# Attention as a 16-step pipeline per sequence, with the maxima as a 97th contraction row, in a one-core attention and mixture-of-experts layer

## The reference

```python
x = x + layernorm(attention(layernorm(x)))     # 16 query heads of 32, one key head and one value head, causal
x = x + layernorm(moe(layernorm(x)))           # 8 experts of 352, the best 2 per token, plus one shared expert of 1408
# attention: q = x @ q_w.T + q_b (16 heads); k, v = one head each
#   scores = q @ k.T / sqrt(32); keys after the query: -inf; softmax over keys; @ v; @ o_w.T + o_b
```

## Time and profile before

| | us |
|---|---|
| median of 3 runs (lowest, highest) | 2210.64 (2209.67, 2216.05) |
| the profiled execution, its own time | 2211.64 |
| the profiled execution, its span | 2209.9 |
| attention, routing, experts, shared expert and end | 0 to 829, to about 860, to 1445, to 2210 |
| busy in the span: TensorE, VectorE, ScalarE, GpSimd | 2059.7, 1141.1, 704.0, 465.8 |

### The profile page before, as it was taken

One profiled execution on the slowest core, in us unless ns is written; L12 is line 12 of the kernel. 1 busy time (PEld: TensorE's weight loads), 2 busy tenths in 40 slices (PEclk: granted clock), 3 DMA queues, 4 the chain that ended last, 5 costly groups with the idle time before them and its releaser, 6 DMA issues. The chain is left out here.

```text
span 2209.9 us, 32623 instructions
## 1 busy us (share of the span) xinstructions
PE 2059.7 (93%) x11754; PEld 1604.8 (73%) x11754; DVE 1141.1 (52%) x2253; ACT 704.0 (32%) x1254; POOL 465.8 (21%) x885
## 2 busy tenths in 40 slices
PE   5999999999999953799999999989999999999995
PEld 4666676766667633677788788878888888888884
DVE  4766758577675738444445555444433424334243
ACT  3425345353543420344444444332111111111111
POOL 1323414142341420211101111001012021120212
PEclk9999999999999975899999999999999999999998
DMA  5043261414415112444434545333022020220202
GB/s 172 31 119 114 62 174 38 136 54 120 128 48 153 39 57 79 172 156 154 154 141 180 211 143 195 109 105 100 19 76 95 19 76 19 76 95 19 76 20 95
DMA packets 104418, 222.76 MB, mean 101 GB/s; under 512 B 9472, under 2 KB 23552, under 8 KB 101152
## 3 DMA queue, kind: packets, MB, share of 16 engines
q1 hardware_dynamic: 92832, 184.14, 25.4%
q0 software_dynamic: 11520, 37.76, 5.4%
HBM read 157.37 MB, written 62.91 MB: 100 GB/s over the span
## 5 line engine op out<-in xcount | busy, mean ns | idle before, releaser
L1121 PE MATMUL ex_bank<-ex_xT,ex_gu 128*128 128x512 f32 (+14 forms) x1656 | 345.1, 367 | 5.4 <-DVE ex_xT L1155 5.4
L1121 PEld LDWEIGHTS ex_bank<-ex_xT,ex_gu 128*128 128x128 f32 (+1 forms) x1656 | 276.8, 182 | 69.9 <-DVE ex_xT L1155 5.9
L1171 DVE TENSOR_TENSOR sh_silu<-sh_silu,sh_bank 128x512 f32<-128x512 f32 x88 | 60.5, 688 | 444.6 <-ACT sh_silu L1164 444.6
L627 DVE TENSOR_REDUCE at_nmax<-at_bank 128x1 f32<-128x384 f32 (+3 forms) x512 | 216.5, 472 | 108.3 <-PE at_bank L431 108.2
L777 ACT ACTIVATE at_PT<-at_bank 128x512 f32<-128x512 f32 (+1 forms) x384 | 187.5, 526 | 265.0 <-PE at_bank L483 258.6
L1121 PE MATMUL sh_bank<-sh_xT,sh_gate 128*128 128x512 f32 x1056 | 256.3, 392 | 4.1 <-DVE sh_xT L1155 4.1
L1133 PE MATMUL sh_bank<-sh_dn,sh_act 128*128 128x512 f32 x1056 | 255.1, 390 | 0.0
L1121 PE MATMUL sh_bank<-sh_xT,sh_up 128*128 128x512 f32 x1056 | 253.9, 389 | 0.0
L837 POOL TENSOR_TENSOR at_minus_max<-idf,at_nmax 128x512 fp32r<-128x512 f32 x128 | 134.1, 1048 | 503.2 <-DVE at_nmax L627 484.9
L1164 ACT ACTIVATE sh_silu<-sh_bank 128x512 f32<-128x512 f32 x88 | 52.6, 598 | 586.4 <-PE sh_bank L1121 586.4
L1121 PEld LDWEIGHTS sh_bank<-sh_xT,sh_gate 128*128 128x128 f32 x1056 | 199.8, 189 | 45.9 <-DVE sh_xT L1155 4.3
(11 more groups left out here) (229 smaller groups left out, 2818.7 us busy)
## 6 DMA issues: line engine op xcount, KB each, us to landing
ex_gu_in<-gu_in SPq DMA_DIRECT2D x23, 1408.0 KB, 9.3
at_Qs<-q_dram SPq DMA_DIRECT2D x96, 256.0 KB, 5.7
ys<-sh_yk SPq DMA_DIRECT2D x17, 1024.0 KB, 5.7
q_dram<-at_q_h SPq DMA_DIRECT2D x64, 256.0 KB, 4.1
ex_dn_in<-dn_in SPq DMA_DIRECT2D x23, 512.0 KB, 9.9
at_x_in<-x_in SPq DMA_DIRECT2D x8, 1024.0 KB, 9.6
at_x_res<-x_in SPq DMA_DIRECT2D x8, 1024.0 KB, 6.6
x<-at_y SPq DMA_DIRECT2D x8, 1024.0 KB, 8.4
```

The costliest lines, as they stand in the source:

```text
L627: last = nc.vector.tensor_reduce(nmax[:, s % 3, i:i + 1], S_ps[u][:, col:col + (i + 1) * P], AX_X, ALU.max, negate=True)
L1121: last = self.nc.tensor.matmul(self.gate_up_ps[c % 2][which][0:m, 0:w], cols(i, k), self.xT[j][:, k, 0:w], start=(step == 0), stop=(step = ...
L1171: nc.vector.tensor_tensor(silu[c % 2][0:m, 0:w], silu[c % 2][0:m, 0:w], gate_up_ps[c % 2][1][0:m, 0:w], ALU.mult).then_inc(s["product"], 1)
```

## The change

It rewrites the attention stage as one pipeline: a turn is 16 steps, one per head, and every engine's stream has the same step structure. Work of one head is spread over steps s (scores, maxima), s + 1 (the maxima's way to a row), s + 2 (scores by key) and s + 3 (exponentials). Everything else of a turn is a "filler" in one of the 16 steps: it goes through one bank (`F_ps`), so that each filler waits until the one before it was taken. A turn b holds heads of sequence b, the output projection of b - 1, the transposes and projections of b + 1, and the router of b - 2, so ten turns are run for eight sequences (two, a loop, and four written out).

- The negated maxima [128 queries, 4] are transposed by TensorE, copied by ScalarE to a row (`row`), and moved by a DMA on ScalarE's queue into a 97th row of `Qs`; `KsT` has ones in its 97th row. The ones matmuls (L483), the diagonals (L837) and the mask matmul of the transposed scores (L479) go.
- GpSimd zeroes the exponentials of later keys instead (`affine_select`, two per head, 384 + 128 columns), and makes the low half of the mixed values in VectorE's place.
- Sums and values share one bank (`AV_ps`). The sums are transposed by VectorE in 32 x 32 blocks, one reciprocal of 16 columns is taken, and a second transpose spreads it.
- There are two copies of the keys, `KsS` for scores by query and `KsT` for scores by key, both moved by ScalarE's queue, when the old ones have been read. Queries are moved per quarter as heads become free.
- The halves of the transposed normalized x1 are stored to DRAM (`xnT`, 2 MB per sequence) and the shared expert loads them into two sets of buffers, in place of loading rows, transposing and splitting.

The diff, cut to its core:

```diff
+        SUM_STEP = {9: 0, 13: 1, 1: 2, 3: 3}
+        MIX_STEP = {10: 0, 14: 1, 2: 2, 4: 3}
+        Q_STEP = {12: 0, 13: 1, 15: 2, 0: 3}
...
         def turns(engine, turn):
-            turn(0, True, False)
-            with engine.Fori(1, NB - 1) as b:
-                turn(b, False, False)
-            turn(NB - 1, False, True)
+            turn(0)
+            turn(1)
+            with engine.Fori(2, NB - 2) as b:
+                turn(b)
+            for b in range(NB - 2, NB + 2):
+                turn(b)
...
+            def transpose_maxima(n, h):
+                pe.wait_ge(max_ready, 3 * (H * n + h) + 3)
+                nc.tensor.transpose(AV_ps[0:QT, 0:P], nmax[:, h % 2, :], idf[:]).then_inc(rows_ps, 1)
...
+            def key_scores(n, h, before):
+                if h == 0:
+                    pe.wait_ge(kT_moved, 48 * n + 48)
+                pe.wait_ge(row_moved[h % 2], 8 * H * n + 16 * (h // 2) + 16)
+                for tb, tiles in enumerate(T_UNITS):
+                    if has(before[0]):
+                        pe.wait_ge(pt_ready, 3 * (H * before[0] + before[1]) + tb + 1)
+                    for j, col in tiles:
+                        w = (QT - j) * P
+                        last = nc.tensor.matmul(T_ps[tb][:, col:col + w], KsT[:, j * P:(j + 1) * P], Qs[:, h, j * P:S],
+                                                start=((j, col) == tiles[0]), stop=((j, col) == tiles[-1]))
+                    last.then_inc(shifted, 1)
...
         @block.tensor
...
+            def turn(b):
+                for s in range(H):
+                    n, h = head(b, s, 1)
+                    if has(n):
+                        m, g = group(b, s - 1, SUM_STEP)
+                        k, f = group(b, s - 1, MIX_STEP)
+                        if g is not None:
+                            pe.wait_ge(sums_taken, C * m + g + 1)
+                        elif f is not None:
+                            pe.wait_ge(mixed_taken, C * k + f + 1)
+                        elif has(head(b, s, 2)[0]):
+                            pe.wait_ge(row_taken, H * head(b, s, 2)[0] + head(b, s, 2)[1] + 1)
+                        transpose_maxima(n, h)
+                    if has(b):
                         query_scores(b, s)
+                    first_filler(b, s)
+                    begin_values(b, s)
+                    second_filler(b, s)
+                    end_values(b, s)
+                    transpose_v(b, s)
+                    n, h = head(b, s, 2)
+                    if has(n):
+                        key_scores(n, h, head(b, s, 3))
...
+            def take_sums(b, s):
+                n, g = group(b, s, SUM_STEP)
+                if g is not None:
+                    dve.wait_ge(summed, C * n + g + 1)
+                    nc.vector.transpose(sums_T[:], AV_ps[:]).then_inc(sums_taken, 1)
...
         @block.vector
...
+            def turn(b):
                 for s in range(H):
+                    maximum(b, s, 0)
+                    norm_steps(b, s, 0)
+                    invert_sums(b, s)
+                    maximum(b, s, 1)
+                    norm_steps(b, s, 1)
+                    spread_inverses(b, s)
+                    first_low(b, s)
+                    maximum(b, s, 2)
+                    norm_steps(b, s, 2)
+                    second_low(b, s)
+                    take_sums(b, s)
+                    scale_mixed(b, s)
+                    take_v(b, s)
+                    norm_steps(b, s, 3)
...
+            def move_row(b, s):
+                n, h = head(b, s, 1)
+                if has(n):
+                    act.wait_ge(row_taken, H * n + h + 1)
+                    act.dma_start(Qs[QK:QK + 1, h, :].bitcast(F32),
+                                  row[:, h % 2, :].bitcast(F32)).then_inc(row_moved[h % 2], 16)
...
         @block.scalar
...
+            def turn(b):
+                for s in range(H):
+                    exponentials(b, s, 0)
+                    if s == 2 and has(b) and has(b - 1):
+                        act.wait_ge(shifted, 3 * H * b)
+                        move_k(b, KsT, kT_moved)
+                    take_row(b, s)
+                    high_mixed(b, s)
+                    exponentials(b, s, 1)
+                    move_row(b, s)
+                    first_high(b, s)
+                    exponentials(b, s, 2)
+                    second_high(b, s)
+                    if s == H - 1 and has(b + 1):
+                        act.wait_ge(scores, 3 * H * (b + 1))
+                        move_k(b + 1, KsS, kS_moved)
...
```

## The result

The changed kernel takes 2258.4 us (median of four runs, 2254.7 to 2263.0) against 2211.6 for the kernel before in the same comparison: a ratio of 1.0208, 95% interval 1.0192 to 1.0225, slower by 2.1%. The prediction was 2216.6, range 2180 to 2250. The profiled run spans 2261.2 us; it is the slowest of the four, 4.6 above their median.

The account below looks back on a forecast made before the run. TensorE's instruction stream was taken to bound attention and shared expert, with waits replacing its removed attention work. From 2211.6: +20.9 attention, -12.5 and -2.4 shared expert make 2217.6, less 1.0 to the median: 2216.6 us, range 2180 to 2250.

Parts of the forecast that it names:

- The step that failed: Attention: a falling TensorE clock was no separate case, low only around 20 us idling; longest predicted wait 2.4 us.
- steps 0: First step of an attention turn: keys land 2.4 us into it; with its query projection predicted 8.2 us.
- steps 12: Attention step with a query projection as filler, bound by the loop through VectorE's third maxima: predicted 5.94 us.
- the ends: Attention's first turn 72 us from 42.5, eighth 82, ninth 38, then 38.6 to routing; end 850.1, 20.9 later.
- The steady schedule: Attention's full turns: sixteen step lengths, each worked out from waits and handovers, summing to 97.4 us against 95.9 before.
- VectorE's transposes: Attention steps 3 and 13: VectorE's transpose of sums out of the bank, taken as 0.6 us, bounds 0.36 and 0.93.
- TensorE keeps part of its saving: First rival, attention: with a third of the waits gone 2178.6 us, wholly TensorE-bound 2101; chance 0.33.
- steps 5 to 8: Attention steps with output projection as filler, waiting on VectorE's third maxima: 5.15 us each, 20.6 together.
- Copies land late: Second rival, attention: keys landing in 5.7 us instead of 2.0 add 26 us, giving 2242.6; chance 0.22.
- the three: The two rivals (chances 0.33, 0.22) and the predicted schedule as it stands (0.45, between 2204 and 2228 us).
- The shared expert: Shared expert: seven sets of sixteen transposes go, -12.5 us; shorter wait at its start, -2.4; period 89.8.
- its 17.7 us a turn: Attention: TensorE waits that replace removed work, 79.7 us of work in a predicted turn of 97.4.

Follow-up runs that it names:

- experiment 6: Changed kernel with the next keys issued earlier in step 15 and third maxima and exponentials ahead of the fillers' results (except steps 1, 2, 9, 10): 2176.7 us, ratio 0.9830.
- Experiment 8: Changed kernel with overwritten matmuls filling the waits in step 0, ahead of step 12 and in steps 1 to 8 of turn 0: 2238.3 us, ratio 1.0111.
- experiment 10: Kernel before without the matmuls that shift and mask the transposed scores; diagonals still built and waited for: 2224.6 us, ratio 1.0041.
- experiment 11: Kernel before without the matmuls that shift and mask the transposed scores, and without the diagonals and the waits for them: 2200.9 us, ratio 0.9947.
- experiment 4: Changed kernel with VectorE's third maxima and ScalarE's third exponential ahead of the filler's result, except in steps 1, 2, 9 and 10: 2209.0 us, ratio 0.9978.
- experiment 5: Changed kernel with only VectorE's third maxima ahead of the filler's result, except in steps 1, 2, 9 and 10; ScalarE's order unchanged: 2218.9 us, ratio 1.0018.
- experiment 9: Kernel before with only the normalized halves stored from attention and loaded in the shared expert, transposes and splits there left out: 2204.7 us, ratio 0.9955.
- experiment 12: Changed kernel with early keys, third maxima and exponentials first, step 0's projection ahead of its scores, and turn 0 filled with matmuls: 2180.1 us, ratio 0.9842.
- experiment 1: Changed kernel with eight overwritten matmuls filling step 0's wait for the keys: 2243.7 us, ratio 1.0149.
- experiment 7: Changed kernel with twenty overwritten matmuls before the first scores and three in each of steps 1 to 8 of turn 0: 2260.2 us, ratio 1.0204.

## Why the prediction was wrong

**The step that failed** is the sentence "That the clock falls is no case of its own: it was low where TensorE idled for 20 us ..., and my longest wait is 2.4." It put the clock at nothing, and took one row of before for a bound, without a row in which TensorE idled for less. In this kernel the clock fell around waits of 2.0 to 2.6 us in all seven steps 0 and behind one of 1.2 in five steps 12, and each fall cost 0.7 to 2.3 us in the next twelve matmuls (3.7 to 5.3 us against 2.99). Such a wait was enough, but it did not always do it (steps 12 of turns 3 and 4; turn 7 of experiment 6); by what rule stays open. The Trainium skill has the case on its page "TensorE: Matmul & The Clock Gate", section "A second HAM failure mode: psum-queue depth-cycling": a kernel whose brief idle moments between groups of matmuls made its clock go to and fro between the levels. The trace agrees (0.50 behind a wait of 1.24 us in step 12 of turn 5); I had read the trace of before for long gaps alone.

**How large the failed step was.** At attention's end the miss is 41.8 us. Experiment 8, which kept the waits and filled them, takes off 26.1 of it, by turns: 3.7 in turn 0, 4.9 in turn 1, 15.6 in turns 2 to 6, 1.8 in turn 7, 0.2 in the rest. These are the profiled executions; by the medians the filling is worth 20 us of the whole time, so some 20 to 26 of the 42 us are the clock's. What is left is 15.7 us, and most of it is at the ends, which I had sized in round numbers: the start and turn 0 are 5.8 us over (to 120.3, predicted 114.5), turn 7 5.3 (87.3 against 82), the steady turns 3.1, the tail 1.3. Part of turn 7's is again the clock, 0.50 in most of 768 to 780, which was not filled.

**The steady schedule was right.** 97.4 us predicted, 97.0 to 98.1 measured with the clock held (99.1 in turn 2, where the keys were late). Single steps missed both ways (step 10 by -0.6 to -0.8, step 2 by +0.2 to +0.7, step 14 by -0.3 to -0.5) and cancelled. TensorE's busy share of attention fell to 84%, where I had said some 85%. The keys' wait of 2.4 us was 2.0 to 2.6. VectorE's transposes cost 0.71 and 0.70 us where I took 0.6 (bounds 0.36 and 0.93). The row's copy of 0.27 and its issue of 0.59 us on ScalarE stand as taken; the dispatch of about 50 ns that the prediction cites from the Trainium skill ("DMA: Bandwidth & Descriptors", Anatomy of one DMA, told there of the GpSimd path) and set against that row would have been wrong here.

**The rivals.** (1) "TensorE keeps part of its saving" fell: no steady turn was under 99.7 us. Neither order has a work-bound TensorE once the shifts are gone: it idles 13 us a turn in the changed kernel and 7 to 8 in experiments 10 and 11. In the new order it is the waits for VectorE's maxima that set steps 5 to 8 (5.10 us, and 4.40 without them in experiments 4 and 5), and the clock comes on top. (2) "Copies land late" fell as well, although its time (2242.6) was the closest of the three. The landings say so, as issue to landing in us at the end of each row:

```profile
at_Qs<-q_dram SPq DMA_DIRECT2D x48, 256.0 KB, 4.7
at_KsS<-at_vk_h ACTq DMA_DIRECT2D x12, 64.0 KB, 2.1
at_KsT<-at_vk_h ACTq DMA_DIRECT2D x12, 64.0 KB, 4.7
```

The keys for the scores took 2.1 us, and TensorE waited for a row once, 0.8 us in turn 0. The second copy of the keys did take 4.7 us and cost 0.7 to 1.0 in step 2 of turns 3 to 6.

**The shared expert.** Predicted -14.9 in all, measured -12.2 in the changed kernel and -7.1 in experiment 9. By the stores of the outputs its turns alternate: 90.0 us, then 91.0 or 91.3 in the changed kernel and up to 94.2 in experiment 9, where I had 89.8 for all. Stalls like those of experiment 12 stand in the longer ones.

**What an engineer could have had instead.** The change's structure is sound; two small orders spoil it. The keys' copies stood behind the filler's result on ScalarE, and the third maxima and exponential stood behind it on VectorE and ScalarE. The prediction worked out the waits that both cause, as part of its 17.7 us a turn, and treated them as given. With both mended, the change is worth 1.7% (experiment 6).

## What to carry to other kernels

Taking work off the busiest engine is worth its time only where that work is not what hides a handover: list, for each removed piece, who is waited for when it is gone. On TensorE a wait can have a second price, the clock, so a schedule with 13 us of short waits in a turn of 100 has to be costed at both levels; filling a wait with matmuls whose result is overwritten tells within one run how much of a slowdown is the clock, and filling it with useful work (the projection ahead of the scores) takes away the wait as well. And in each engine's queue put first what the next step waits for, then what drains a bank: here that order alone was worth 49 us of 2258.

## What was not expected of the hardware

- The kernel before, with 16.2 us of matmuls a turn left out and nothing added, was 0.4% slower: turns of 98.9 us against 95.9, granted clock 0.88 against 1.00, with no wait over 1.6 us in four turns; the clock was at 0.50 behind waits of 0.85 and 0.60 us and at 1.00 around waits of 1.60 and 1.26 (experiment 10).
- Eight extra matmuls in a wait made a step 2.1 us shorter on average (10.7 to 8.6, turns 1 to 7; experiment 1).
- The same wait of 1.2 us ahead of step 12 brought the clock down in turns 2, 5 and 6 and not in 3 and 4 (7.4 to 7.6 us against 5.96), and in turns 0 to 6 all alike in a kernel that differed only in turn 0 (experiment 7).
- A wait of 2.24 us for the keys left the clock at 1.00, and one of 2.16 brought it down (experiment 6).
- In the shared expert's loop TensorE stood idle for up to 2.5 us at a time without anything to wait for in the trace (experiment 12).
